# Routing of the experts moved into the rounds of the small attention before them

## What is computed

```python
# L0_ffn: one expert of 8 per token
logits = xf @ gate_w + gate_b
one_hot = jax.nn.one_hot(jnp.argmax(logits, axis=-1), E, dtype=xf.dtype)
h = jax.nn.gelu(jnp.einsum('td,edh->teh', xf, w1), approximate=True)
y = jnp.einsum('teh,ehd->ted', h, w2)
out = jnp.einsum('te,ted->td', one_hot, y)

# L1_ffn: two experts of 8 per token
probs = jax.nn.softmax(xt @ gate_w + gate_b, axis=-1)
top_v, top_i = jax.lax.top_k(probs, K)
combine = jnp.sum(jax.nn.one_hot(top_i, E, dtype=xt.dtype) * top_v[..., None], axis=1)
for e in range(E):
    h = jax.nn.gelu(xt @ W1[e] + b1[e], approximate=False) @ W2[e] + b2[e]
    out = out + combine[:, e:e + 1] * h
```

## Time and profile before

| | us |
|---|---|
| median of 3 runs | 4944.34 (4937.5 to 4951.55) |
| span of the profiled execution | 4944.1 |
| first expert layer, first instruction to first fetch | 79.4 |
| third expert layer, the same | 103.5 |
| round of the small attention, L0 / L1 | 17.6 / 18.2 |

### The profile page before, as it was taken

One profiled execution on the slowest core, in us unless ns is written; L12 is line 12 of the kernel. 1 busy time (PEld: TensorE's weight loads), 2 busy tenths in 40 slices (PEclk: granted clock), 3 DMA queues, 4 the chain that ended last, 5 costly groups with the idle time before them and its releaser, 6 DMA issues. The chain is left out here.

```text
span 4944.1 us, 90876 instructions
## 1 busy us (share of the span) xinstructions
PE 3835.4 (78%) x25840; PEld 2735.3 (55%) x25840; DVE 3465.1 (70%) x9524; ACT 2341.8 (47%) x5537; POOL 2386.9 (48%) x3900
## 2 busy tenths in 40 slices
PE   7889797779999799568869937567775887799365
PEld 5666565656666466456646626422332665466265
DVE  7887775666666676566658856669998664588566
ACT  3444464355666466234436624345553454366243
POOL 5666442534344442446643354367776662233453
PEclk9999898789999899679979959779998999899698
DMA  6000332100000232133323311212121330133113
GB/s 234 0 0 1 112 124 76 52 20 1 0 0 1 72 124 94 39 124 107 107 80 117 110 38 47 73 48 65 63 62 64 114 117 28 51 120 112 36 46 87
DMA packets 244547, 341.24 MB, mean 69 GB/s; under 512 B 26976, under 2 KB 187120, under 8 KB 243120
## 3 DMA queue, kind: packets, MB, share of 16 engines
q1 hardware_dynamic: 230960, 309.19, 18.8%
q0 software_dynamic: 13184, 27.22, 1.6%
HBM read 182.77 MB, written 147.26 MB: 67 GB/s over the span
## 5 line engine op out<-in xcount | busy, mean ns | idle before, releaser
L522 DVE TENSOR_REDUCE l0att_rowmax<-l0att_S 128x2 f32<-128x512 f32 x512 | 339.8, 687 | 125.2 <-PE l0att_S L701 122.9
L893 POOL TENSOR_TENSOR wb_prob<-wb_prob,wb_rden 128x128 f32<-128x128 f32 (+1 forms) x512 | 248.2, 506 | 360.7 <-DVE wb_rden L1070 360.3
L522 DVE TENSOR_REDUCE l1ffn_rowmax<-l1ffn_S 128x2 f32<-128x512 f32 x512 | 337.6, 686 | 87.2 <-PE l1ffn_S L701 83.1
L1983 POOL TENSOR_TENSOR ssm_hc<-core_AW_all,ssm_Cs 128x512 f32<-128x512 f32 x256 | 320.8, 1268 | 131.2 <-DVE core_AW_all L2129 98.1
L1434 POOL DMA_INDIRECT results<-e_y,e_back x220 | 213.7, 971 | 289.4 <-DVE e_y L1662 269.9
L935 ACT ACTIVATE wb_prob<-wb_biased,wb_nmax 128x128 f32<-128x128 f32 (+1 forms) x512 | 228.6, 447 | 236.0 <-DVE wb_nmax L1063 233.6
L2228 PE MATMUL ssm_Y<-ssm_hc,core_ident 128*128 128x512 f32 x512 | 287.8, 672 | 56.8 <-POOL ssm_hc L1983 31.1
L2129 DVE TENSOR_TENSOR_SCAN core_AW_all<-core_AW_all,ssm_U 128x512 f32<-128x512 f32 x256 | 310.6, 1213 | 1.0 <-ACT core_AW_all L2072 0.6
L701 PE MATMUL l1ffn_S<-l1ffn_K,l1ffn_Q 128*128 128x512 f32 x512 | 251.0, 494 | 75.1 <-DVE l1ffn_rowmax L522 42.3
L1775 PE MATMUL e_H<-e_xT,e_W1s 128*128 128x128 f32 x1760 | 252.0, 288 | 70.2 <-issue 50.6
L701 PE MATMUL l0att_S<-l0att_K,l0att_Q 128*128 128x512 f32 x512 | 248.6, 489 | 60.4 <-DMA l0att_K<-bounce 47.5
(11 more groups left out here) (498 smaller groups left out, 11511.3 us busy)
## 6 DMA issues: line engine op xcount, KB each, us to landing
bounce<-l0att_parts SPq DMA_DIRECT2D x128, 256.0 KB, 2.8
bounce<-l1ffn_parts SPq DMA_DIRECT2D x128, 256.0 KB, 2.8
ssm_Cs<-c_rows SPq DMA_DIRECT2D x128, 256.0 KB, 3.1
routed<-core_Y SPq DMA_DIRECT2D x8, 2048.0 KB, 24.8
l0att_Q<-bounce SPq DMA_DIRECT2D x128, 128.0 KB
l0att_K<-bounce SPq DMA_DIRECT2D x128, 128.0 KB
bounce<-l1att_parts SPq DMA_DIRECT2D x64, 256.0 KB, 2.8
l1ffn_Q<-bounce SPq DMA_DIRECT2D x128, 128.0 KB
```

Of the source, the lines that this page charges most:

```text
L522: dve.tensor_reduce(out=rowmax[:, jp, qt, 2 * pair:2 * pair + 2], in_=S[a % 2][:].rearrange("p (j k) -> p j k", j=2)[:, :, 0:keys(qt)], op ...
L893: ins = pool.tensor_tensor(out=prob[:, w_ % NP, a:b], in0=prob[:, w_ % NP, a:b], in1=rden[:, w_ % NP, n:n + 1].to_broadcast([P, b - a]), o ...
L1983: pool.tensor_tensor(out=hc[:, u % 4], in0=hs[:, u % 4], in1=Cs[:, n % 4], op=ALU.mult)\
```

## The change

The routing leaves `experts` and becomes part of the small attention before it, which is told by `route` how many experts a token takes (`top`), whether the tokens are normalised first, and the gate. Two pieces join the plan of a round r: at slot 8 gh, the transposition of sequence r-2's finished rows, and at slot 14 gl, its logits. The choice is made in five batches of 3, 4, 4, 3 and 2 sequences (`BATCHES`), three rounds after a batch's last sequence: DVE's steps of it are a generator (`choosing`), of which one step is run after each slot. One round later with two experts, in the same one with one, stands gr at slot 12, the ranks, and after it the generator `locating`. `scatter` on POOL sends one sequence per round, its first tile ahead of the second preparation of maxima and its second tile behind `part`, from the round after its batch was placed. `ROUNDS` goes to 17. What isn't done then, the last batch among it, is done behind the rounds, and `tables` too; SP waits for all rows there. With one expert the normalised rows are made by POOL twice, once for gh and once for the scatter; with two, POOL copies the rows, where ACT did before.

In `experts` nothing is left ahead of the first fetch but the load of the bias `b2`. A row's number is now a float, and `give` takes the larger of it and a spare number in one operation. Scratch of the routing lies in buffers of the dense layer's weights; those are now loaded in the state-space layer, and the second wide attention's weights between the fetches of the first expert layer.

```diff
         if rope:
...
             plan = {3: "mt1", 4: "v", 5: "n0", 6: "n1", 7: "h", 9: "qk", 10: "on", 11: "mt0", 13: "out"}
...
-        ROUNDS = range(-3, SEQS + 1)
+        R = route
+        ROUNDS = range(-3, SEQS + (2 if R else 1))
+        BATCHES = ((0, 3), (3, 4), (7, 4), (11, 3), (14, 2))
+        RANK_AT, EXP_AT, LAGS = 12, 4, 3
+        chosen_in, ranked_in = {}, {}
+        if R:
+            plan.update({8: "gh", 14: "gl"})
+            ahead.update({"gh": -2, "gl": -2})
+            for b, (first, many) in enumerate(BATCHES):
+                if first + many - 1 + LAGS + R.top - 1 in ROUNDS:
+                    chosen_in[first + many - 1 + LAGS] = b
+                    ranked_in[first + many - 1 + LAGS + R.top - 1] = b
+        late = [b for b in range(len(BATCHES)) if b not in chosen_in.values()]
...
+            def normalise_rows(n):
...
+                pool.wait_ge(g_var.sem, g_var.at(n))
+                own.step(pool.tensor_tensor(out=grstd[:, at], in0=gve[:], in1=core.minus_half[:, 0:QT], op=ALU.pow))
...
+                for t in range(QT):
+                    k = n * QT + t
+                    ins = pool.tensor_scalar(xn[:, t, :], core.Y[:, k, :], gmv[:, k, 0:1], grstd[:, k:k + 1],
+                                             ALU.subtract, ALU.mult)
+                ins.then_inc(g_normed.sem, 1)
+
+            def scatter(n, t):
...
+                pool.wait_ge(g_placed.sem, g_placed.at(b))
+                await_(pool, rows_sent[n % 2], sends(n - 2) if n >= 2 else 0)
+                if R.normed_in:
+                    own.step(pool.tensor_scalar(mine[:, 0, 0:D], core.Y[:, k, :], gmv[:, k, 0:1], grstd[:, k:k + 1],
+                                                ALU.subtract, ALU.mult))
+                else:
+                    own.step(pool.tensor_copy(mine[:, :, 0:D], core.Y[:, k:k + 1, :].to_broadcast([P, R.top, D])))
+                    own.step(pool.tensor_copy(mine[:, :, D + 1:D + 2], gweight[:, b % 2, :, i:i + 1]))
+                own.step(pool.tensor_copy(mine[:, :, D:D + 1], core.numbers[:, 0:R.top, k:k + 1]))
+                own.settle()
+                for x in range(R.top):
+                    pool.indirect_dma_start(
...
+            def scatter_due(r):
+
+                n = scattered
+                first, many = BATCHES[batch_of(n)] if inside(n) else (SEQS, 1)
+                return R and inside(n) and r >= first + many - 1 + LAGS + R.top
...
                 if inside(r + 3):
                     normalise(r + 3)
+                normalise_rows(r - 2)
+                due_now = scatter_due(r)
+                if due_now:
+                    scatter(scattered, 0)
                 hide(r, 0, 8)
                 if inside(r + 1):
                     part_max(r + 1, 0)
...
                 last(r + 3)
+                if due_now:
+                    scatter(scattered, 1)
+                    scattered += 1
                 if out_norm and inside(r - 1):
                     out_power(r - 1)
+            if R:
+                for n in range(scattered, SEQS):
+                    for t in range(QT):
+                        scatter(n, t)
...
+                    if R and R.normed_in:
+                        for at, part in ((15, 0), (0, 1), (1, 2)):
+                            n = r - (1 if part == 0 else 2)
+                            if u == at and inside(n):
+                                gauge(n, part)
+                    if u == 0 and r in chosen_in:
+                        routing = chain(routing, choosing(chosen_in[r]))
+                    if u == RANK_AT and r in ranked_in:
+                        routing = locating(ranked_in[r])
+                    next(routing, None)
+            if R:
+                for _ in routing:
+                    pass
+                for b in late:
+                    for _ in choosing(b):
+                        pass
+                    take_ranks(b)
+                    for _ in locating(b):
+                        pass
+                tables()
...
+                elif x == "gh":
+                    if R.normed_in:
+                        pe.wait_ge(g_normed.sem, g_normed.at(n))
+                    else:
+                        pe.wait_ge(fed.sem, fed.at(n))
+                    claim(x, n)
+                    for t in range(QT):
+                        src = xn[:, t, :] if R.normed_in else core.Y[:, n * QT + t, :]
+                        ins = pe.transpose(F[:, tile(t)], src, core.ident[:])
+                elif x == "gl":
+                    out_of(pe, "gh", n)
+                    claim(x, n)
...
-                run(dve.tensor_tensor(out=back[:, j % RING, 0:1], in0=number(got[:, j % RING, D:D + 1]),
-                                      in1=keep_i[:, j:j + 1].bitcast(U32), op=ALU.bitwise_and))
-                dve.tensor_tensor(out=back[:, j % RING, 1:2], in0=back[:, j % RING, 0:1],
-                                  in1=spare_i[:, j:j + 1].bitcast(U32), op=ALU.bitwise_or).then_inc(back_ready.sem, 1)
+                dve.tensor_tensor(out=back[:, j % RING, 0:1], in0=got[:, j % RING, D:D + 1], in1=spare[:, j:j + 1],
+                                  op=ALU.max).then_inc(back_ready.sem, 1)
```

614 lines of the change are left out of this document (327 added, 287 removed).

## The result

The changed kernel takes 4744.91 us (median of 4 runs, 4741.39 to 4749.07) against 4944.34 for the kernel before (median of three runs): a ratio of 0.960, 95% interval 0.9589 to 0.9613. A fourth run of the kernel before took 5411.59 us, is in a slower state and is not compared. The forecast was 4811 with a range down to 4755; the sign was right, the gain half again as large. The profiled execution took 4741.39 with a span of 4739.7 us, 204.4 less than before.

A forecast was written before the change was run, and what follows sets the result against it. The prediction took four serial routing stretches, about 366 us with no engine near its limit, as pure delay. 4944.1 - 186 (stretches less tails) + 76 (rounds) - 23 (routed loop) = 4811 us, range 4755 to 4900.

The forecast's parts named there:

- The tail: Between small attention and first routed fetch: POOL's queue sets what remains; 44 us saved per L0 layer, 49 per L1, -186 together.
- The rounds: Small attention's rounds, which take in the moved routing work: 14 us longer per L0 layer, 24 per L1, +76 for four layers.
- What enters the rounds: Prediction's part pricing work added to PE, DVE, ACT and POOL in the small attention's rounds: +76 us for four layers.
- lower end: Rounds with the added work hidden where PE's waits cover it: at least 7.7 us per L0 layer and 15 per L1 layer.
- the pieces: gh, gl and L0's statistics in the rounds: by the low estimate 5.3 us per L0 layer and 8.0 per L1 layer.
- the scatters: POOL's two tiles a round: below the round's length, so costed at nothing; without that cover 22 us per L0 layer.
- gh stands at slot 8 behind the K transfer, so neither wait of rows 4 covers it: PE's waits for K transfer and DVE's row maximum don't hide gh: 14 x 0.38 = 5.3 us per layer.
- The price of the batches: gr and DVE's choice steps, costing where DVE is late: 0.8 us per batch in L0, 2.3 in L1; 2.4 and 6.9 per layer.
- The loop: Loop over routed tiles, one DVE operation fewer: 0.17 us x 71 tiles x 2 L1 layers, -23 us; L0 nothing, PE setting the pace.
- No room in the rounds: Rival, chance 0.12: every added instruction in the rounds is exposed, 148 us instead of 76, giving 4883 us.
- Each new entry costs a hand-over: Rival, chance 0.05: PE stands at gh, gl and gr for unready input or bank, 161 us on top, 4972 us.
- DVE stands for POOL: Rival, chance 0.10: DVE's two-input batch steps in the rounds wait for POOL's SBUF instructions, 54 us more, 4865 us.

## Why the prediction was wrong, step by step

**The tail** was right: POOL's queue, 44 us saved per L0 layer and 49 per L1 layer were forecast, 42.3, 44.5, 51.3 and 51.8 measured. The tiles were a little cheaper and the way from the last issue to the fetch 1.5 to 1.8 us longer. The sum is off by 4 of 186 us.

**The rounds** are where it failed: +76 forecast, +28.2 measured, 48 of the 71 us by which the span fell short of 4811. (The rest is 8 in the loops, 4 in the tails and 11.6 in "all else"; with the rounds alone as measured the forecast would have been 4763, inside its range.) Two steps of the part "What enters the rounds" are at fault.

The first is the choice between the ends: "Both engines take their instructions in order and two more entries share the two banks, so I don't take the lower end". That put 30.6 us on top of a lower end of 2 x 7.7 + 2 x 15 = 45.4. There is nothing in the runs for it. The mechanism named, entries that queue at the banks, doesn't show: with gh and gl in the rounds and the choices behind them, two more entries a round cost 3.7 and 2.5 us in the L0 layers, everything else of the pieces included, and -0.4 and 0.3 in the L1 layers; and PE waits at neither in the steady rounds.

The second is that the lower end itself was too high by 17 us: the pieces were 20.5 us too dear, the scatters 3.9 too cheap. "gh stands at slot 8 behind the K transfer, so neither wait of rows 4 covers it" looks only at the wait that comes before the piece. A wait that comes after it covers it as well: in L1 PE waits for DVE's maximum behind gh at slot 9 and behind gl at slot 0, and these waits shrink by what is added, 18.1 us of them in 12.7 rounds having become 12.3. In L1 DVE sets the pace (five steps that wait for each other cost nearly their full time at slot 4 too), so what is added to PE is free there. And the durations were taken for prices. The two transpositions of gh have a duration of 0.38 us, as in the earlier trace rows, but in L0 the next product starts 0.14 us after the first of them (PE, L0; in the L1 round 0.52 us pass, 2675.84 to 2676.36, and there it is the wait that covers them):

```profile
815.80 0.38 PE L1041 MATMUL l0att_F<-core_ident,core_w 128*128 128x128 f32 x2
815.94 0.82 PE L1087 MATMUL l0att_T<-l0att_Q,l0att_K 128*128 128x256 f32 x4
```

On DVE it is the same, here in a round of L1 with steps of a batch:

```profile
2682.42 0.22 DVE L854 TENSOR_TENSOR core_w<-l1ffn_F,core_dispatch 128x64 f32<-128x64 f32 x1
2682.55 0.22 DVE L868 TENSOR_TENSOR core_w<-core_w 128x64 f32<-128x64 f32 x1
2682.68 0.69 DVE L669 TENSOR_REDUCE l1ffn_rowmax<-l1ffn_S 128x2 f32<-128x512 f32 x1
```

Starts are 0.13 us apart at a duration of 0.22. The Trainium skill, VectorE: DVE Perf Modes, section The DRAIN you can't avoid, says that the next operation does not start until the pipe is empty, that one that is not held starts earlier, and that a semaphore in between costs nothing extra. The trace agrees with the second, 0.09 and 0.13 us between starts where nothing waits. The third is not what these short operations show: 0.24 us apart with a wait at each, though those are wider too.

The price of the batches came out at 18.4 us against 18.6, as I read it by luck, by errors that cancel: a step costs 0.11 to 0.14 us where 0.2 was taken, but in L1 all 30 of them count and not 11 or 12 (3 x 30 x 0.11 to 0.14 is 10 to 13 us for each of these layers, of which 4.3 and 7.1 were measured, so part of them is still covered).

**The loop.** In L1 -23 was forecast and -19.2 measured. "In L0 PE sets the pace and I count nothing" missed 12.0 us. PE sets the pace on three tiles of four; on the fourth POOL adds tensors and DVE's one-element operation lasts 1.74 us instead of 0.14, as in the row for L1 (1.22). Before, in the first expert layer (DVE, POOL and PE):

```profile
934.29 1.74 DVE L1652 TENSOR_TENSOR e_back<-e_got,e_keep_i 128x1 uint32<-128x1 uint32 x1
934.74 1.27 POOL L1438 TENSOR_TENSOR core_X<-core_X,core_Y 128x512 f32<-128x512 f32 x1
...
936.07 0.16 DVE L1654 TENSOR_TENSOR e_back<-e_back,e_spare_i 128x1 uint32<-128x1 uint32 x1
...
936.82 0.43 DVE L1645 COPY e_W1s<-core_W 128x512 f32 x1 [0.33 <-issue]
...
937.35 0.91 PE L1775 MATMUL e_H<-e_xT,e_W1s 128*128 128x128 f32 x6 [0.36 <-issue]
```

and after:

```profile
902.18 1.72 DVE L1816 TENSOR_TENSOR e_back<-e_got,core_w 128x1 uint32<-128x1 f32 x1
902.60 1.27 POOL L1737 TENSOR_TENSOR core_X<-core_X,core_Y 128x512 f32<-128x512 f32 x1
...
904.09 0.41 DVE L1809 COPY e_W1s<-core_W 128x512 f32 x1
...
904.74 1.06 PE L1887 MATMUL e_H<-e_xT,e_W1s 128*128 128x128 f32 x8
```

Before, the weights' copy ends at 937.25 and PE, idle for 0.36 us, goes on at 937.35; from its first product to the next tile's first such a tile takes 2.43 us and the next one 1.97, where the others take 1.90. After, DVE stands as long beside POOL, but with one operation less its copy ends at 904.50 and PE goes on without a gap: 1.90 on nearly every tile. Seven and eight such tiles at 0.6 are 4.2 and 4.8 us of the 6.8 and 5.2 by which the two loops got shorter.

**The rivals.** "No room in the rounds" (4883) and "Each new entry costs a hand-over" (4972) fall with the kernels above. "DVE stands for POOL" is real in the loop, where both engines read two tensors from SBUF, but not in the rounds: taking all of POOL's scatters out changed them by -0.7 to -2.7 and +1.4 us, and 3.9 us more of POOL's scalings a round cost 2.0 us in all. Nor do the additions of the earlier trace rows show it: in 26 of the 30 a POOL instruction was under way at the same time, in 22 of them a scaling that reads SBUF, and none took over 348 ns.

Of the signs that the prediction named, the tails were seen (38 us from the last addition in L0 and 54 from the last power in L1, where 36 and 53 were said), and in the steady rounds PE waits at gh and gl for nothing. The L1 tiles of 2.1 us were half seen: where POOL adds nothing, tiles of 2.05 and 2.30 alternate, and before all took 2.29. The rounds of 18.4 and 19.6 us were not seen: from one sequence's first maximum to the next one's, the kernel after needs 0.5 us more than before in L0 and 0.6 in L1 (mean of twelve rounds in each of the two layers), where the forecast had 0.8 and 1.4.

## What to carry to other kernels

Work that is moved under another engine's pace cost here the distance between starts, not the duration of its rows, and a wait of the engine behind the place of the work covered it as well as one before it; so price it from the engine that sets the pace, and test which that is by putting a known load at two places. A serial tail that is left is the queue of one engine: count its instructions, and ask how early it is fed before making the pieces smaller. Cut the traces into stretches before comparing medians, since a stretch that the edit doesn't touch can move by as much as the edit.

## What the runs showed of the hardware

The second wide attention is a loop in the programs of the engines. In the kernel with 39 more operations ahead of it DVE stands at the loop's end, between L1433 and L1443, where the kernel after goes straight on (L1430 and L1440 there). The profile puts the wait down to PE's products, but the last of those before DVE goes on end at 1226.99 us, 0.74 us earlier. First the kernel with the shifted code, then the kernel after:

```profile
1224.52 0.69 DVE L1433 TENSOR_TENSOR wb_V<-wb_F,core_w 128x512 f32<-128x512 f32 x1 [0.85 <-PE wb_F L1532]
1227.73 0.29 DVE L1443 CUSTOM_DVE_ANT_0 wb_biased<-wb_S,wb_added 128x128 f32<-128x128 f32 x1 [2.52 <-PE wb_S L1548]
```

```profile
1211.53 0.69 DVE L1430 TENSOR_TENSOR wb_V<-wb_F,core_w 128x512 f32<-128x512 f32 x1 [0.85 <-PE wb_F L1529]
1212.44 0.29 DVE L1440 CUSTOM_DVE_ANT_0 wb_biased<-wb_S,wb_added 128x128 f32<-128x128 f32 x1 [0.22 <-PE wb_S L1545]
```

In this attention (990 to 1640 us in the one, 985 to 1610 in the other) the queue that loads code moved 39 packets of 8 KB in the one and 15 in the other (queue, packets, MB, share):

```profile
q14 instruction: 39, 0.32, 0.2%
```

```profile
q14 instruction: 15, 0.12, 0.1%
```

Most of these 15 stand at the attention's two ends. From 1150 to 1520 us, inside the loop, the kernel with the shifted code loads 22 packets, one of them at 1225.6 while DVE stands as shown above, and the kernel after loads none:

```profile
q14 instruction: 22, 0.18, 0.2%
```

```profile
DMA packets 0, 0.00 MB, mean 0 GB/s; under 512 B 0, under 2 KB 0, under 8 KB 0
```

In five of the fifteen stretches of 64 score products the shifted kernels need 43 to 45 us instead of 40. A pass of the loop has two such stretches, and the loop branches back five times (the first and the last pass stand outside it), so DVE stands at every branch back, and not in every second pass as the expectation said. The kernels with 1339 to 1341 executed DVE instructions between the first attention of L0 and this loop, and the kernel before with 1471, don't have it; those with 1368, 1380 (two kernels), 1411 and 1414 do. The Trainium skill, Runtime: NRT & Kernel Launch, section Instruction fetch mechanics, says that a taken branch whose target is not in the window at hand forces a fetch before execution goes on. The trace agrees, at about 4 us for each of the five stretches; that the place in the code decides it was shown by the one kernel that only moves the code.
